# Windowed attention in a fused whitening, attention and expert kernel: value tiles by transfers from stored rows, the band mask on GpSimd, attention output in two PSUM banks

## The reference, cut to what matters

```python
# x: (16, 56, 56, 64) float32
x = whiten(x) * gamma + beta            # groups of 16 channels, 5 Newton-Schulz steps over all tokens
t = x.reshape(16, 3136, 64)
n = layernorm(t)                        # over the 64 channels
windows = pad(n, 16)[:, i : i + 33]     # each token sees itself and 16 neighbours on both sides
attn = softmax(n . windows / 8)         # 33 scores of a token
t = t + layernorm(sum(attn * windows)) * gamma1 + beta1
t = t + moe(layernorm(t))               # 8 experts 64-64-64, the best 2 of each token
```

## Time and profile before

| | |
|---|---|
| median of 3 runs | 1167.22 us |
| profiled execution | 1171.15 us, of which the span from first to last instruction is 1169.3 us |
| PE busy | 1100.4 us (94%) |
| DVE busy | 909.2 us (78%) |
| ACT busy | 611.7 us (52%) |
| POOL busy | 146.7 us (13%) |
| mean granted TensorE clock | 0.958 of 2.4 GHz |
| second stage | from about 80 us to about 590 us of the span |

### The profile page before, as it was taken

How to read it: one execution, slowest core, us unless ns; L and a number is a source line. 1 busy time by engine, 2 the same in 40 slices (tenths; PEclk the granted TensorE clock), 3 DMA queues, 4 the chain that set the end, 5 groups by cost and what they waited for, 6 DMA issues and landing times.

```text
span 1169.3 us, 28068 instructions
## 1 busy us (share of the span) xinstructions
PE 1100.4 (94%) x9550; PEld 739.6 (63%) x9550; DVE 909.2 (78%) x2575; ACT 611.7 (52%) x975; POOL 146.7 (13%) x173
## 2 busy tenths in 40 slices
PE   7858999999999999998789999999999999999998
PEld 7836777777777777777554555555555555555553
DVE  6943678888888888888678887887777777887875
ACT  0014566666666666665245555555555555555553
POOL 6021222222222222222100000000000000000000
PEclk9957899999999999999569999999999999999999
DMA  9501112122121212111012222222222222222221
GB/s 285 212 16 33 49 49 62 52 60 55 57 57 56 58 50 61 53 57 41 24 47 60 67 71 70 67 68 70 71 66 67 71 71 67 68 70 69 67 67 48
DMA packets 136196, 79.18 MB, mean 68 GB/s; under 512 B 112417, under 2 KB 134177, under 8 KB 135345
## 3 DMA queue, kind: packets, MB, share of 16 engines
q1 hardware_dynamic: 127040, 64.78, 21.3%
q10 hardware_dynamic: 8064, 12.85, 2.9%
q0 software_dynamic: 1008, 0.43, 0.2%
HBM read 52.33 MB, written 25.69 MB: 67 GB/s over the span
## 4 chain that ended last, share of the span: by engine, by line
PE 79%; ACT 8%; DVE 6%; issue 3%; SPq 2%; DMA 1%; POOL 0%; DVEq 0%; ACTq 0%; POOLq 0%
PE p L1096 16%; PE p L1071 15%; PE p L1081 9%; PE p L1045 6%; PE p L916 5%; PE p L1011 5%; PE p L1023 4%; ACT prob L515 4%; PE p L909 4%; PE p L926 3%; ACT xt_s L459 3%; PE p L1040 2%; PE p L1092 2%; PE p L924 2%; DVE arena L603 1%
## 5 line engine op out<-in xcount | busy, mean ns | idle before, releaser
L532 ACT ACTIVATE arena<-p,b_s 128x896 f32<-128x896 f32 x224 | 225.3, 1007 | 246.9 <-PE p L1071 246.1
L825 DVE TENSOR_TENSOR arena<-arena,p 128x896 f32<-128x896 f32 x224 | 242.7, 1083 | 93.0 <-PE p L1081 89.8
L1096 PE MATMUL p<-arena,w_s 128*64 128x448 f32 x896 | 215.7, 560 | 0.3 <-DVE arena L825 0.3
L1071 PE MATMUL p<-thl,w_hi 128*128 128x448 f32 x448 | 164.9, 449 | 0.4 <-DVE thl L799 0.4
L1081 PE MATMUL p<-arena,selector 128*128 128x448 bf16 x448 | 124.7, 360 | 3.5 <-DVE arena L825 3.0
L1081 PEld LDWEIGHTS p<-arena,selector 128*128 128x128 bf16 x448 | 25.5, 97 | 161.6 <-issue 116.1
L1071 PE MATMUL p<-thl,w_lo 128*128 128x448 f32 x448 | 127.5, 366 | 0.0
L723 DVE TENSOR_REDUCE sm<-sq 128x14 f32<-128x896 f32 (+1 forms) x59 | 61.3, 1038 | 66.7 <-ACT sq L486 58.7
L1071 PEld LDWEIGHTS p<-thl,w_hi 128*128 128x128 f32 x448 | 85.8, 192 | 21.3 <-issue 1.0
L418 POOL TENSOR_TENSOR yb<-yb,bet 128x448 f32<-128x448 f32 x56 | 59.2, 1058 | 290.5 <-DVE xn_s L766 290.5
L1071 PEld LDWEIGHTS p<-thl,w_lo 128*128 128x128 f32 x448 | 85.0, 190 | 7.2
(11 more groups left out here) (174 smaller groups left out, 1793.8 us busy)
## 6 DMA issues: line engine op xcount, KB each, us to landing
tn_spill<-tnt_s ACTq DMA_DIRECT2D x56, 224.0 KB, 1.9
arena<-tn_spill SPq DMA_DIRECT2D x56, 224.0 KB, 3.4
t_s<-tn_spill SPq DMA_DIRECT2D x56, 224.0 KB, 2.5
arena<-in_x_dram SPq DMA_DIRECT2D x112, 96.0 KB, 2.1
out_dram<-arena SPq DMA_DIRECT2D x112, 96.0 KB, 1.8
resid<-in_x_dram SPq DMA_DIRECT2D x6, 1568.0 KB, 13.5
resid<-in_x_dram SPq DMA_DIRECT2D x6, 384.0 KB, 7.0
arena<-in_x_dram SPq DMA_DIRECT2D x112, 16.0 KB, 2.0
```

The source lines that it names most:

```text
L532: a.activation(hid[:, j % 2, :].rearrange("p (h n) -> p h n", h=H), (p34 if j % 2 == 0 else p56)[:, :, 0:CH], ACT.Gelu, bias=b1_s[:, j:j + ...
L825: v.tensor_tensor(gated[:, j % 2, :].rearrange("p (h n) -> p h n", h=H), hid[:, j % 2, :].rearrange("p (h n) -> p h n", h=H), p01[:, :, 0: ...
L1071: last = t.matmul(bank[:, h, 0:CH], w[:, 128 * j:128 * (j + 1)], thl[:, c, h, :], start=(k == 0), stop=(k == 1))
L1096: last = t.matmul(p2[64 * h:64 * h + 64, 0:CH], w2_s[:, j, :], gated[:, j % 2, h * CH:(h + 1) * CH], start=False, stop=(j == 3))
```

## The change

- The transposes L1023 and the copies L492 go. Instead SP stores each xn tile to a DRAM array `xn_rows` in token order, padded with 16 zero rows at both ends of an image pair (3 transfers a tile), and reads the 96-row windows back as value tiles (2 transfers a tile, one for each image) into `v_a` for even tiles and `v_b` for odd ones. The windows of tile q need rows of tile q+1 too.
- The products L1040 go. After the exponential POOL multiplies the 96x896 tile `prob` by the 0/1 band, as the first instruction of its step, and PV waits for that.
- PV goes to bank `p7` for even tiles and to the first bank of `p56` for odd ones, and waits for t of two tiles before, no longer of the tile before. The transposes of tn go to the other bank of `p56`, no longer into the bank of x.
- xn is overwritten (DVE) only after its rows are stored. Four transfers that zero the pads are issued by POOL at the start.

```diff
+    rows_xn = nc.dram_tensor("xn_rows", (NP, WIN + TOK + WIN, H, C), f32).ap()
+        values = [v_a[:, :, :, :], v_b]
+        def windows(n, at_q, h):
+            return bass.AP(rows_xn.tensor, (n * (TOK + 2 * WIN) + at_q) * H * C + h * C,
+                           [[H * C, KEYS], [BLK * H * C, NB], [1, C]])
+        def sums(q):
+            return (p7 if q % 2 == 0 else p56[:, 0])[:, 0:NB * (C + 1)]
...
+            def rows_out(q):
+                at_q = WIN + q % CPI * CH
+                to = rows_xn[q // CPI, at_q:at_q + CH]
+                sp.wait_ge(s_xn, q + 1)
+                sp.dma_start(to[0:TAIL].rearrange("(b p) h c -> p b (h c)", p=128),
+                             xn_s[:, 0:NB - 1, :].rearrange("p (b h) c -> p b (h c)", h=H)).then_inc(s_xw, 16)
+                for h in range(H):
+                    sp.dma_start(to[TAIL:, h], xn_s[64 * h:64 * h + 64, NB - 1, :]).then_inc(s_xw, 16)
+            def values_in(q):
+                at_q = q % CPI * CH
+                sp.wait_ge(s_xw, 48 * min(q + 2, G))
+                wait(sp, s_o, q - 1)
+                for h in range(H):
+                    sp.dma_start(values[q % 2][:, :, h, 0:C], windows(q // CPI, at_q, h)).then_inc(s_vd[q % 2], 16)
+            for g in range(G + 1):
+                if g < G:
+                    rows_out(g)
+                if g + 3 < G:
+                    tokens_in2(g + 3)
+                if g > 0:
+                    values_in(g - 1)
...
+            for half in range(2):
+                for edge in (0, WIN + TOK):
+                    pool.dma_start(rows_xn[half * (NP // 2):(half + 1) * (NP // 2), edge:edge + WIN].rearrange("n p h c -> p n (h c)"),
+                                   zeros.rearrange("p (n c) -> p n c", n=NP // 2)).then_inc(s_pad, 16)
...
             def step(g, c, has):
+                if has(2):
+                    q = g - 2
+                    wait(pool, s_p, q + 1)
+                    if has(3):
+                        wait(pool, s_t2, q - 1 if has(4) else 0)
+                    if has(1):
+                        wait(pool, s_yb, q + 1)
+                    scores = prob[:, :, :].rearrange("p h (b n) -> p (h b) n", b=NB)
+                    v.tensor_tensor(scores, scores, band[:, :].unsqueeze(1).to_broadcast([KEYS, H * NB, BLK]),
+                                    ALU.mult).then_inc(s_pm, 1)
...
-                if has(2):
-                    q = g - 2
-                    wait(act, s_vt, q + 1)
-                    wait(act, s_o, q)
-                    a.activation(v_s[:, :, :, 0:C].rearrange("p b h c -> p (b h) c"),
-                                 p56[0:KEYS].rearrange("p a (n c) -> p (a n) c", c=C)[:, 0:NB * H, :], ACT.Copy).then_inc(s_vs, 1)
...
                     wait(dve, s_xnt, g)
+                    wait(dve, s_xw, 48 * g)
...
-                    wait(pe, s_p, q + 1)
-                    wait(pe, s_vs, q + 1)
-                    wait(pe, s_t, q)
+                    wait(pe, s_pm, q + 1)
+                    pe.wait_ge(s_vd[q % 2], 32 * (q // 2 + 1))
+                    wait(pe, s_t, q - 1)
...
-                    for b in range(NB):
-                        at_b = cq * CH + b * BLK
-                        last = t.transpose(p56[0:KEYS, b // 4, (b % 4) * 128:(b % 4 + 1) * 128],
-                                           keys_t[:, at_b:at_b + KEYS], eye[:, :])
-                    last.then_inc(s_vt, 1)
...
-                    for h in range(H):
-                        t.matmul(p34[0:KEYS, h, 0:CH], eye_h[0:KEYS, 0:KEYS], outside[:, 0:CH], start=True, stop=False)
```

More of the change, by code:

```diff
@@ L217, in hybrid_kernel @@
         s_xnt, s_kts = sem("xn_t"), sem("keys_copied")
-        s_vt, s_vs, s_s, s_p, s_o = sem("v"), sem("v_copied"), sem("scores"), sem("probs"), sem("pv")
+        s_pad, s_xw, s_vd = sem("pads_zeroed"), sem("xn_rows_stored"), [sem(f"values_in{i}") for i in range(2)]
+        s_s, s_p, s_o = sem("scores"), sem("probs"), sem("pv")
+        s_pm = sem("probs_masked")
         s_sqy, s_sq, s_t = sem("y_squared"), sem("pv_squared"), sem("t_scaled")
@@ L304, in _, with tokens_in2 @@
                 load(n)
[L306 to L312, removed]
+            def tokens_in2(g):
+                wait(sp, s_xt, g - 2)
+                for tile, tokens in pieces(x_tokens, g, x2[:, SLOT3[g % 7], :]):
+                    sp.dma_start(tile, tokens).then_inc(s_x2[g % 7], 16)
+            def rows_out(q):
[12 more added lines that the diff above has]
+                    sp.dma_start(values[q % 2][:, :, h, 0:C], windows(q // CPI, at_q, h)).then_inc(s_vd[q % 2], 16)
+            for g in range(3):
+                tokens_in2(g)
+            sp.wait_ge(s_pad, 16 * 4)
+            for g in range(G + 1):
[5 more added lines that the diff above has]
+                    values_in(g - 1)
             sp.wait_ge(s_xt, G)
@@ L409, in _ @@
             pool.wait_ge(s_prep, 1)
+            v.memset(v_b[:, :, :, C], 1.0)
             v.memset(keys_t[:, 0:WIN], 0.0)
@@ L413, in step @@
             def step(g, c, has):
+                if has(2):
[8 more added lines that the diff above has]
+                                    ALU.mult).then_inc(s_pm, 1)
                 if has(1):
                     q, cq = g - 1, prv(c, 1)
+                    if has(2):
+                        wait(pool, s_pm, q)
                     wait(pool, s_xn, g + 1 if has(0) else G)
@@ L423, in step @@
                     wait(pool, s_yb, q + 1)
+                    if has(2):
+                        wait(pool, s_pm, q + 2)
                     if has(4):
@@ L1010, in step @@
                             b, h = (cell // 2 * 2 + half, cell % 2) if cell < NB - 1 else (cell, half)
-                            last = t.matmul(p7[64 * half:64 * half + 64, cell * (C + 1):(cell + 1) * (C + 1)],
-                                            prob[:, h, b * BLK:(b + 1) * BLK], v_s[:, b, h, :], start=True, stop=True)
+                            last = t.matmul(sums(q)[64 * half:64 * half + 64, cell * (C + 1):(cell + 1) * (C + 1)],
+                                            prob[:, h, b * BLK:(b + 1) * BLK], values[q % 2][:, b, h, :], start=True, stop=True)
                     last.then_inc(s_o, 1)
-                if has(2):
-                    q, cq = g - 2, prv(c, 2)
-                    wait(pe, s_kts, q + 2 if has(1) else q + 1)
-                    wait(pe, s_vs, q)
-                    if isinstance(q, int) and q == 0:
-                        pe.wait_ge(s_zero, 2)
-                    for b in range(NB):
-                        at_b = cq * CH + b * BLK
-                        last = t.transpose(p56[0:KEYS, b // 4, (b % 4) * 128:(b % 4 + 1) * 128],
-                                           keys_t[:, at_b:at_b + KEYS], eye[:, :])
-                    last.then_inc(s_vt, 1)
                 if has(5):
```

37 lines of the change are left out of this document (19 added, 18 removed).

## The result

The changed kernel takes 1320.3 us, the median of 4 runs (1318.59 to 1321.15), against 1167.78 for the kernel before (1163.54 to 1168.4): ratio 1.131, 95% interval 1.128 to 1.134. That is 153 us slower. The forecast was 1253, with a range of 1134 to 1284: the sign was right, but the loss is nearly twice the one forecast, and the time lies outside the range.

The account below looks back on a forecast made before the run. PE was taken to bound the 8.50 us step, with a ring of 8.05 close behind. 50 x (10.2 - 8.5) = +85 on 1171, minus 4 for the median, +1 for filling and draining: 1253 us, range 1134 to 1284.

Parts of the forecast that it names:

- The ring: Dependency loop PV, ACT's square, DVE statistics, ACT's exponential, `xt_s`, y, transposes of xn, PV: 8.05 us a step.
- the block: DVE instruction with two SBUF inputs waits for POOL's mask to end: L740 starts 1.83 us later each step.
- PE relieved, ring closes, no mask: 1.32 us a step removed from PE, of which the ring lets 0.45 through: 22 us on 50 steps.
- the clock term: PE idle 2.95 us a step lowers the clock some third of the time: step 10.2 us, between 9.88 and about 10.9.
- the blocked ring: The ring with DVE's wait for the mask in it: 8.05 + 1.83 = 9.88 us a step.
- PE's own work: PE's work in a new step without its waits and the removed transposes and mask products: 6.93 us.
- The second rival: No block of DVE, but PE's idle 1.12 us a step lowers the clock: about 1180 us; chance 0.10.
- The first rival: Neither engine blocks, or POOL waits, and the clock holds: step 8.05 us, 1137 us; chance 0.24.
- nothing there: Two banks free PV from waiting for t: no gain in the steady step, up to 5 us in draining.
- the third rival: Value transfers land late and PE waits before PV: step 9.55 us, 1215 us; chance 0.06.
- The fourth rival: Only small blocks of DVE, a few tenths: step 8.4 to 8.6 us, about 1167 us; chance 0.08.

Follow-up runs that it names:

- e4: Changed kernel plus 12 fillers a step (throwaway bf16 products on PE ahead of y, overwritten by it): 1222.35 us, ratio to before 1.048.
- e5: Changed kernel with the mask left out (output lacks the band) and 4 throwaway PE products (fillers) a step: 1138.07 us, ratio to before 0.976.
- e10: Changed kernel, mask still on POOL, plus 6 throwaway PE products (fillers) a step: 1233.77 us, ratio to before 1.058.
- e7: e4 with POOL's mask replaced by an 8-column product and two memsets (no mask in the output): 1183.03 us, ratio to before 1.017.
- e2: Changed kernel with the mask left out altogether, no fillers (output lacks the band): 1197.72 us, ratio to before 1.023.
- e1: Changed kernel with the mask back on PE as products, value transfers and two banks kept: 1154.65 us, ratio to before 0.990.
- e9: e6 with PV waiting for t of the tile before again, so the second bank is of no use: 1154.65 us, ratio to before 0.994.
- e6: Changed kernel with the mask back on PE and 2 throwaway PE products (fillers) a step: 1136.18 us, ratio to before 0.977.
- e3: Kernel before with only the mask moved to POOL; value transposes, copies and single bank stay: 1286.5 us, ratio to before 1.103.
- e8: Changed kernel with POOL's mask waiting for xn of its step, plus 6 throwaway PE products (fillers): 1234.25 us, ratio to before 1.061.

## Why the prediction was right in its sign and wrong in its size

With e4 and e5 the loss splits into the three terms of the sum. The ring without mask at full clock is e5 against before, the block e4 against e5, the clock the changed kernel against e4. The last two hold only as far as e4's fillers cost nothing. By the steps of e10 at full clock the block is 9.20 - 8.00 = 1.20 us a step (60 us) and the clock 11.46 - 9.20 = 2.26 (113 us), so the true block lies near or below the 84 of the table and the clock near or above the 97. The ratios of the table, each against before on its own chip, are multiplied by 1168:

| term | forecast, us | measured, us |
|---|---|---|
| PE relieved, ring closes, no mask | 50 x (8.05 - 8.50) = -22 | 0.976: -28 |
| block of DVE by the mask | 50 x 1.83 = +92 | 1.048 - 0.976: +84 |
| granted clock | 50 x 0.32 = +16 | 1.131 - 1.048: +97 |
| sum | +86 | +153 |

- **The step that failed is the clock term**, "with the clock down for some third of the time, 10.2". It should have been 11.46 for 9.60, that is 1.9 us a step and not 0.32. The path was wrong too: the forecast kept the blocked ring as what bounds the step and let the clock only stretch it, while in 17 of 32 steps the runs show PE's own work at the low clock, 11.6 us without a gap, longer than the blocked ring. Even the upper end taken from the earlier trace rows, 10.9, was too low. Those rows span one step, from 117.64 to 128.50 us, whose clock is 0.50 only up to about 122.9, so they did not bound a step that runs at the low clock throughout. The way to a bound was open: at the low clock PV takes 1.73 for 1.04, and the 6.93 us of own work in that ratio are 11.5.
- **The block was right in mechanism and nearly in size.** With the clock held the step is 9.60 (e4) or 9.20 (e10) against 9.88: 1.2 to 1.6 us for 1.83. The operation named, L740's, is caught in 15 of 37 steps of e4. In the changed kernel it is caught in 2 of 32, L738's in 11, and L757's in 17, since PE and with it the exponential come later. The prediction allowed for L757, but said that xn would then be late; in the changed kernel it is not. The Trainium skill, "SBUF — State Buffer", section "Who interferes with whom", says that a VectorE instruction with two SBUF inputs contends with a GpSimd instruction that reads SBUF, but not with one that only writes. The trace agrees on both halves: 2.05 us for 0.17 beside the mask, 0.17 beside the memset of e7.
- **The second rival was a true mechanism, only not alone.** Waits of PE of at most 1.1 us each, without any block, cost 55 us (e2 against e5). Its price, 1180 us, was near the 1198 measured. I had it beside the forecast with 0.10, though the forecast contained a longer idle time than the rival did. The two should not have been priced apart. The Trainium skill, "TensorE: Matmul & The Clock Gate", section "A second HAM failure mode: psum-queue depth-cycling", has a kernel whose clock swings because PE idles briefly and often between its groups; e2 and e1 agree, with 0.76 and 0.95. Short idle times alone do not do it, though: e4 has 0.54 us a step, and the second half of e10 1.3, at 1.00.
- **The first rival,** 1137 us, was worked out right (e5, 1138.07), and its condition did not hold.
- **Two banks: "nothing there" was wrong.** They are worth some 18 us once the rest runs at 8.0 (e9 against e6). In the earlier trace rows PE has no idle time before PV, and I took that for slack; but the trace of the kernel before has t end only 0.14 us ahead of PV:

```profile
356.73 1.43 DVE L772 SCALAR_TENSOR_TENSOR t_s<-p,sm,gam 128x64 f32<-128x64 f32 x7
...
358.30 0.40 PE L1011 MATMUL p<-v_s,prob 96*64 96x65 f32 x6
```

  So two thirds of the 0.45 us that the ring was said to let through needed the second bank: without it the step is 8.35.
- **PE's own work** was put at 6.93 us a step. In e7, where PE never stands still, the 12 fillers (recorded in one group) start 2.32 us ahead of y's bias, and a step is 8.92. That leaves 6.6 of own work. The estimate was 0.3 too high, and PE's idle time as much too low:

```profile
304.57 2.48 PE L1052 MATMUL p<-bet_rows,ones_h 128*128 128x455 bf16 x12
306.89 0.36 PE L981 MATMUL p<-bet_rows,ones_h 128*128 128x455 bf16 x1
```

- **The values are hidden**, so the third rival falls. In the changed kernel a value transfer lands in 3.4 us, for which I had 3.1, and PE is never seen waiting for one:

```profile
v_a<-xn_rows SPq DMA_DIRECT2D x56, 168.0 KB, 3.4
```

  The only such waits in any run are four of e9, 2.0 us in all, and one of e6, 0.9 us. The fourth rival, small blocks, falls with e4: they are 2 us.

What stays open: why the clock of the changed kernel stands at 0.64 and that of e3 at 0.88, when the mask is the same. It is not the idle time of a step by itself: e3 has more of it (1.9 us for 1.4), in three waits, where a step of the changed kernel has one or none. That e3's PE has more work in each step fits too, but no run varies PE's work, its idle time and the way that it is cut up apart. Nor was the mask split in two and placed where DVE has no operation with two SBUF inputs; the time between such operations in the loop is short, as e8 showed.

## What to carry to other kernels

Before work goes to GpSimd, list VectorE's instructions with two SBUF inputs that can fall in its time, however small: a 0.17 us link of a dependency ring pays GpSimd's whole 2 us, and moving the GpSimd instruction past the ring may only bring it against the next such link. Work taken off TensorE is a gain only if no idle time is left in its place; where a step keeps even 0.7 us of it, price the step at the lower clock as well, by PE's whole own work and not only by the ring, and try a few throwaway products in the gap (two a step gave 1.3% here). An engine without idle time before an instruction says nothing of the slack of what that instruction waits for: read when each of its inputs was ready.

## What the runs showed of the hardware

- The mean granted clock from 130 to 500 us beside PE's idle time a step: 1.00 with 0.49 us (e9) and 0.54 (e4), 0.95 with 0.69 (e1), 0.76 with 0.77 (e2), 0.64 with 1.4 (the changed kernel), but 0.88 with 1.9 (e3) and 1.00 with 1.3 (e10 from 310 us on). The idle time a step does not put the clocks in order.
- A mean like 0.64 or 0.76 is made of whole stretches at either level. From 393.4 to 405.0 us the changed kernel ran at 0.50, the 1.2 GHz level, with PE busy throughout, and a step took 11.6 us for the 6.6 of own work at 2.4 GHz.
- With GpSimd writing only, VectorE's two-input operations were untouched, but its fp32 copy of 392 columns took 0.80 us (e7) for 0.36 (e5).
- Which of the two engines is held goes by who was first: the mask was never lengthened (2066 to 2080 ns over 41), but in e8, behind tn's product, the add of beta was (1357 ns on average for 1066).
